# An RNN layer and an LSTM layer in one kernel: a bias load changes its queue, a bias product its place, and the low parts of four weight chunks are made later

## The reference

```python
# layer 0, residual
h = tanh(h @ WhR + (x_t @ WxR + bR));  y_t = x_t + h
# layer 1, residual
a = (y_t @ WxL + bL) + h @ WhL         # 2048 columns: i, f, o, g
c = sigmoid(f) * c + sigmoid(i) * tanh(g)
h = sigmoid(o) * tanh(c);  out_t = y_t + h
```

## Time and profile before

| | us |
|---|---|
| median of 3 runs | 891.57 |
| profiled execution | 892.13 |
| its span | 890.3 |
| TensorE busy | 863.1 (97%) |
| VectorE busy | 746.1 (84%) |
| ScalarE busy | 397.8 (45%) |
| GpSimd busy | 223.4 (25%) |
| granted TensorE clock | 0.997 |

### The profile page before, as it was taken

One profiled execution on the slowest core, in us unless ns is written; L12 is line 12 of the kernel. 1 busy time (PEld: TensorE's weight loads), 2 busy tenths in 40 slices (PEclk: granted clock), 3 DMA queues, 4 the chain that ended last, 5 costly groups with the idle time before them and its releaser, 6 DMA issues.

```text
span 890.3 us, 42241 instructions
## 1 busy us (share of the span) xinstructions
PE 863.1 (97%) x18576; PEld 507.8 (57%) x18576; DVE 746.1 (84%) x1964; ACT 397.8 (45%) x1064; POOL 223.4 (25%) x503
## 2 busy tenths in 40 slices
PE   5999999999999999999999999999999999999996
PEld 4455656555565565555655655555556555565642
DVE  4679888888888888888888888888888888888874
ACT  2746334444444444444444444444444444444431
POOL 1111122222222222222222222222222222222210
PEclk9999999999999999999999999999999999999998
DMA  8901100111100011110011110001111000000000
GB/s 308 264 3 26 27 15 15 26 27 27 27 24 17 16 27 27 27 27 14 15 27 27 27 27 14 22 20 27 27 27 27 15 3 15 15 15 15 15 14 14
DMA packets 38649, 30.06 MB, mean 34 GB/s; under 512 B 4268, under 2 KB 37184, under 8 KB 37184
## 3 DMA queue, kind: packets, MB, share of 16 engines
q1 hardware_dynamic: 38044, 27.16, 10.9%
q10 hardware_dynamic: 420, 0.20, 0.1%
HBM read 18.95 MB, written 8.39 MB: 31 GB/s over the span
## 4 chain that ended last, share of the span: by engine, by line
PE 87%; DVE 6%; DMA 2%; SPq 2%; issue 2%; ACT 1%; POOL 0%; POOLq 0%; DVEq 0%
PE ps_l L783 36%; PE ps_l L809 31%; PE ps_r L848 8%; PE ps_r L865 8%; DMA wxl_raw<-in_L_cond_Wx 2%; PE ps_l L798 2%; SPq L271 1%; DVE pre_l L614 1%; ACT gates L424 1%; DVE h_lo L649 1%; DVE h_hi L636 1%; PE ps_r L823 1%; PE ps_r L833 1%; ACT tanh_c L431 1%; DVE c L625 1%
## 5 line engine op out<-in xcount | busy, mean ns | idle before, releaser
L809 PE MATMUL ps_l<-wxl_hi,whl_raw 128*32 128x512 f16 x3840 | 251.2, 379 | 0.0
L809 PEld LDWEIGHTS ps_l<-wxl_hi,whl_raw 128*32 128x32 f16 x3840 | 104.2, 97 | 103.5 <-issue 4.9
L315 POOL TENSOR_TENSOR xb<-xb,h_l 128x128 f32<-128x128 f32 x128 | 59.2, 462 | 328.4 <-DVE h_l L642 328.4
L783 PE MATMUL ps_l<-whl_hi,hT_hi 128*32 128x512 f16 x2016 | 130.8, 379 | 3.9 <-DVE hT_hi L640 3.1
L338 POOL TENSOR_TENSOR yT<-xT,hT_r 128x128 f32<-128x128 f32 x128 | 58.6, 458 | 295.6 <-DVE hT_r L682 295.6
L783 PE MATMUL ps_l<-whl_hi,hT_lo 128*32 128x512 f16 x2016 | 130.6, 379 | 0.0
L783 PE MATMUL ps_l<-whl_lo,hT_hi 128*32 128x512 f16 x2016 | 130.6, 379 | 0.0
L614 DVE SCALAR_TENSOR_TENSOR pre_l<-ps_l,g_products,bias_l 128x256 f32<-128x256 f32 x240 | 105.1, 479 | 26.1 <-PE ps_l L783 19.5
L809 PE MATMUL ps_l<-wxl_lo,whl_raw 128*32 128x512 f16 x1920 | 125.6, 379 | 0.0
L665 DVE SCALAR_TENSOR_TENSOR pre_r<-ps_r,g_products,xr 64x128 f32<-64x128 f32 x224 | 78.4, 350 | 34.1 <-POOL xr L328 29.1
L436 ACT ACTIVATE h_r<-pre_r 128x128 f32<-128x128 f32 x128 | 39.6, 310 | 134.5 <-DVE pre_r L665 106.6
(11 more groups left out here) (108 smaller groups left out, 1277.4 us busy)
## 6 DMA issues: line engine op xcount, KB each, us to landing
out<-xb SPq DMA_DIRECT2D x128, 64.0 KB, 1.8
xb<-in_x SPq DMA_DIRECT2D x126, 64.0 KB, 2.1
whl_raw<-in_L_cond_Wh SPq DMA_DIRECT2D x4, 1024.0 KB, 14.4
wxl_raw<-in_L_cond_Wx SPq DMA_DIRECT2D x4, 1024.0 KB, 15.9
wxr_raw<-in_L_cond_Wx SPq DMA_DIRECT2D x1, 1024.0 KB, 7.1
whr_raw<-in_L_cond_Wh SPq DMA_DIRECT2D x1, 1024.0 KB, 9.0
xb<-in_x ACTq DMA_DIRECT2D x2, 64.0 KB, 4.8
h0n<-in_cond ACTq DMA_DIRECT2D x1, 64.0 KB
```

The costliest lines, as they stand in the source:

```text
L315: nc.gpsimd.tensor_tensor(xb[g % NX][:, t, :], xb[g % NX][:, t, :], h_l[s % 2][:, :], ALU.add).then_inc(out_done, 1)
L783: last = nc.tensor.matmul(ps_l[s % 2][quarter(j), :], (hT_hi, hT_lo)[h_part][:, k, :], gate_slice(whl[w_part][k], j), start=False, stop=(h ...
L809: last = nc.tensor.matmul(ps_l[s % 2][quarter(j), :], y16[y_part][g % 2][:, k, t * B:(t + 1) * B], gate_slice(wxl[w_part][k], j), start=(y ...
```

## The change

Three edits.

1. The load of the LSTM bias goes from SyncE's queue to ScalarE's, and there the order becomes: two quarters of x, LSTM bias, h0.
2. TensorE does the LSTM bias product right behind the RNN one, ahead of `product_r(0)`; ScalarE waits once, for both, before it copies them.
3. The low parts of the input matrix: chunk 0 in turn 10 instead of 9, chunk 1 in turn 11 instead of 10, chunks 2 and 3 both in turn 12 instead of 11 and 12.

```diff
-        W_LOW_AT = {6: [(OF_H, 1), (OF_H, 2)], 7: [(OF_H, 3)], 9: [(OF_X, 0)], 10: [(OF_X, 1)], 11: [(OF_X, 2)], 12: [(OF_X, 3)]}
+        W_LOW_AT = {6: [(OF_H, 1), (OF_H, 2)], 7: [(OF_H, 3)], 10: [(OF_X, 0)], 11: [(OF_X, 1)], 12: [(OF_X, 2), (OF_X, 3)]}
...
             sp.dma_start(bias_rows_r, bR.rearrange("(j u) -> j u", j=J)).then_inc(s_bias_r, DMA)
-            sp.dma_start(bias_rows_l.rearrange("j (g u) -> j g u", g=G),
-                         bL.rearrange("(g j u) -> j g u", g=G, j=J)).then_inc(s_bias_l, DMA)
             sp.dma_start(wr_raw[OF_X][:, :], WxR.rearrange("(p k) n -> p (k n)", k=J)).then_inc(s_wr[OF_X], DMA)
...
         def _(act):
+            load_x(act, 0, (2, 3))
+            act.dma_start(bias_rows_l.rearrange("j (g u) -> j g u", g=G),
+                          bL.rearrange("(g j u) -> j g u", g=G, j=J)).then_inc(s_bias_l, DMA)
             act.dma_start(h0n[:, :], h0.rearrange("b (j u) -> j b u", j=J)).then_inc(s_h0, DMA)
-            load_x(act, 0, (2, 3))
...
-            act.wait_ge(bias_mm, 1)
+            act.wait_ge(bias_mm, 2)
             nc.scalar.activation(bias_r[:, :], ps_l[0][:, 0:P], ACT.Copy).then_inc(bias_done, 1)
-            act.wait_ge(bias_mm, 2)
             nc.scalar.activation(bias_l[:, :], ps_l[1][:, :], ACT.Copy).then_inc(bias_done, 1)
...
             nc.tensor.matmul(ps_l[0][:, 0:P], spread_j, bias_rows_r, start=True, stop=True).then_inc(bias_mm, 1)
-            product_r(0)
             pe.wait_ge(s_bias_l, DMA)
             nc.tensor.matmul(ps_l[1][:, :], spread_j, bias_rows_l, start=True, stop=True).then_inc(bias_mm, 1)
+            product_r(0)
```

## The result

| | before | after |
|---|---|---|
| median, us | 891.85 (891.12 to 892.18, 4 runs) | 898.58 (897.94 to 898.69, 4 runs) |
| profiled execution, us | 892.13 | 898.72 |
| its span, us | 890.3 | 896.9 |

The ratio is 1.0076, 95% interval 1.0057 to 1.0093: 6.7 us slower, clear of noise, where 1.3 us were forecast, with 894.1 as the upper end of the range.

The account below looks back on a forecast made before the run. The bound was a chain: DMA landing until 38.73 us, TensorE until 97.9, VectorE with ScalarE until 116.5, then TensorE. Terms -0.31 + 0 + 0 + 1.65 = +1.34 us gave a median of 892.9 us, range 891.0 to 894.1.

Parts of the forecast that it names:

- h0's landing: At the front, h0 behind x's quarters and the bias would land at about 9.5 to 10 us, costing nothing.
- the landing at 38.73: At the front, TensorE's `step_0_input` waits until 38.73 us for the last chunk of the LSTM's input matrix.
- Edit 1's gain of 0.31 us: At the front, without the bias load on SyncE's queue the big loads start and land sooner: -0.31 us.
- Edit 2 at 0 us: At the front, the RNN starts about 2 us sooner, but the last input chunk's landing hides it: 0 us.
- turn 9's gain at 0: `cell(4)` could start some 0.3 us sooner, but `cell(5)` cannot, as TensorE's product ends too late: 0 us.
- turn 12's cost of 1.65 us: Two low parts on VectorE delay `y_lo`, TensorE's `product_l(8)` and `cell(7)`: +1.65 us, bounds 0 to 2.27.
- A: Rival, front: the landing isn't set by bytes alone, so 2.07 us more gain comes through; 890.8 us, chance 0.12.
- C: Rival, turn 12: VectorE reaches its two low parts sooner, so their delay vanishes; -0.31 us, 891.3 us, chance 0.08.
- B: Rival, front: the bias load's issue of 0.26 us was hidden, so no gain there; +1.65, 893.2 us, chance 0.14.
- D: Rival, at 97.5 us: TensorE's wait drops its clock to 1.2 GHz, up to 3.6 us more; 896.5, chance 0.04.

Follow-up runs that it names:

- front_only: The changed kernel with the low parts where they were before the change; 896.72 us against 892.06 before.
- h0_on_sync: The changed kernel with low parts as before and h0's load on SyncE's queue ahead of the first 1 MB load; 890.77 us against 891.51 before.
- hold_big: The changed kernel with low parts as before, SyncE waiting for h0 before issuing the first 1 MB load; 892.90 us against 891.51 before.
- order_and_product: The kernel before with x's quarters ahead of h0 on ScalarE's queue and the LSTM bias product ahead of `product_r(0)`; 890.40 us against 891.51.
- order_only: The kernel before with only x's quarters put ahead of h0 on ScalarE's queue; 890.34 us against 892.06 before.
- order_again: The same kernel as order_only, timed again in more rounds; 889.89 us against 891.38 before.
- h0_middle: The changed kernel with low parts as before and ScalarE's queue holding x's quarters, h0, LSTM bias in this order; 893.84 us against 891.38 before.
- low_only: The kernel before with only the low parts moved as in the change; 893.36 us against 892.06 before.
- bias_queue_only: The kernel before with the LSTM bias load moved to ScalarE's queue behind h0 and x's quarters; 891.93 us against 891.38 before.
- low_double_10: The kernel before with low parts 0 and 1 in turn 10, one each in 11 and 12, none in 9; 892.85 us against 891.38 before.
- product_only: The kernel before with only the LSTM bias product put ahead of `product_r(0)`; 892.32 us against 891.51 before.
- h0_first: The changed kernel with h0 issued first on ScalarE's queue, then x's quarters, then the LSTM bias; 894.41 us against 892.06 before.

## Why the prediction was wrong

**The failed step is h0's landing.** I wrote that a quarter of x in that place had landed at 9.41 and "h0 then lands at about 9.5 to 10", and from this that "nothing of this reaches the landing at 38.73". h0 came at 18.35, and a term that the sum held at nothing was +4.99 us at mark 1, +4.66 in front_only's median. Two things were wrong in it. I took over a time of landing from one load to another. What decides it, as far as these runs show, is how much of the queue is still to be fetched when the 1 MB loads begin, and the room that these leave; x's 9.41 was itself such a wait. And I did not see that edit 1 itself moves both ends of the race the wrong way: it puts the bias ahead of h0 (issue at 2.32 us) and starts the first 1 MB load sooner (2.04 instead of 2.45). The runs in one table:

| kernel | h0 issued | first 1 MB load issued | h0 used at |
|---|---|---|---|
| h0_on_sync | 2.03, SyncE | 2.74 | 4.97 |
| hold_big | 2.32 | 5.14 | 5.15 |
| order_and_product | 1.69 | 2.35 | 7.47 |
| order_only | 1.67 | 2.35 | 9.40 |
| order_again | 1.70 | 2.35 | 10.26 |
| h0_middle | 1.68 | 2.02 | 12.98 |
| after | 2.32 | 2.04 | 18.35 |
| front_only | 2.31 | 2.02 | 18.79 |

On ScalarE's queue, issued 0.7 us ahead of the first big load, h0 gets part of its pieces through and comes at 7.5 to 10.3; 0.3 ahead, at 13; behind it, at 18.4 to 18.8. I had cited the Trainium skill, *DMA: Bandwidth & Descriptors*, section "Queues, rings and completion order", which has each DMA engine go round between the queues by packet, and drew from it only that h0 would be late by little. The profile's packets show the size: 26 of q10 against 114 of q1 in 2 us, which isn't one for one.

Only a short stretch of the RNN's delay was free, 1.31 us, and I never asked how much. It would have been the rival to write: RNN steps late by more than the front's cover. I also left out that the peaks of the RNN weights stand behind h0 on VectorE. h0_middle (first recurrent product at 18.09, behind the bias at 14.38) already pays 2.46. Nor was the landing alone the limit of the front before: the chains of low_only, bias_queue_only and low_double_10 begin with x's landing and run through the RNN's steps, not through the last chunk. The two paths were nearly equal there.

**Edit 1's gain of 0.31 us** can't be seen: the first big load was issued 0.41 us sooner, but the stretch behind it was taken over by h0. In bias_queue_only mark 1 came 0.27 sooner and the median 0.55 later; nothing can be told.

**Edit 2 at 0 us** was right: product_only shows no gain, and the product did run in TensorE's idle front (at 4.50). In product_only the first recurrent product came at 12.77, 1.7 us sooner, and TensorE then waited 2.23 us for the last chunk at 39.09.

**Edit 3, turn 9's gain at 0 and turn 12's cost of 1.65 us**, was right. After: +1.60 between the marks; low_only: +1.60 between them and +1.30 in the medians. The wait of the weight loads was 1.79 where 1.63 were forecast, and `y_lo` ended it, as said. Turn 9 went as said too: in low_only `cell(4)` came 19.62 us behind mark 1 instead of 20.01, `cell(5)` 27.40 instead of 27.41.

**The rivals.** A (the RNN's head start comes through) and C (the slip is swallowed) did not happen. B's mechanism was not what cost the front. D fell: behind the wait 16 matmuls took 1.05 us, against 1.04 at 80.70 before. (Its 3.6 us was also a little high: 7.5 us with 1.08 of 1.94 needed loses 3.3.) None of them was the one that came, and the range had no room for it: its upper end was made of the slip alone.

## What to carry to other kernels

A small load on a second queue that the first products need has to be issued well ahead of the big loads of the other queue, or ahead of them in their own queue; otherwise it gets few packets (13 in a microsecond here) and lands several times later than alone (16.0 us against 2.8 here). When loads change places, price each by what will be in flight when it is issued, and count what the edit does to the big loads' start too. A landing that hides a chain covers it only up to a length that has to be read, not assumed.

## What the runs showed of the hardware

- 64 KB in 128 pieces took 2.8 us from issue to use with nothing big in flight, and 16.0 us behind the 1 MB loads of the other queue; 8 KB in 16 pieces took 8.6 us there (h0_first) and 11.5 (h0_middle).
- The first 1 MB load landed 4.9 to 6.5 us behind its issue in the eight kernels with x's quarters first on ScalarE's queue, and 6.4 to 7.7 us behind it in five of the six with h0 first (7.1 before); the sixth, bias_queue_only, has 5.4. By 8 us SyncE's queue had moved 1.42 to 1.55 MB in the four kernels with h0 first and the LSTM bias on SyncE's queue, 1.47 of them before, and 1.65 to 1.94 MB in the others, hold_big aside.
- In order_only the last chunk was in use at 37.30 and in order_again at 36.73 instead of 38.73. The landing alone doesn't make their gain, since in low_double_10, with the loads of before, TensorE had its last wait for a chunk until 37.09. It had reached `step_0_input` at 34.5 to 35.3 us with the front of before (34.87 before, 34.52 in low_double_10, 35.26 in low_only), and reached it at 32.55 in order_only and 32.2 in order_again: the order moves both paths to the front's end.

```profile
16.07 20.62 DMA wxl_raw<-in_L_cond_Wx
36.73 1.06 PE ps_l L761 x8
```

  Why the order of two small loads on one queue moves the start of the stream on the other was not separated: h0's issue took 1.17 us when it came first and x's quarters 0.42 and 0.45, but no run tries one without the other.
- TensorE's granted clock fell to 0.50 (1.2 GHz) for about 3 us in the front of four kernels, front_only from 26 to 29 us and h0_on_sync, hold_big and order_and_product between 27 and 34, with 32 matmuls of 128 columns in 1.94 us instead of 1.08. Before it fell TensorE had been busy for 0.78 us from 22 to 24 (front_only), 0.24 from 24 to 26 (h0_on_sync), 0.65 from 26 to 28 (hold_big) and 0.20 from 24 to 26 (order_and_product). In the last three TensorE still waited 1.4 to 1.5 us for the last chunk, so it did not set the front. In the kernel after the rows give 1.00 throughout, yet 32 matmuls took 1.93 us as late as 24.43; from there to the next `rnn_add` it took 2.00 us against 1.75 before, so slow matmuls are at most a few tenths of the 5 us.
- The same front scatters: h0 in order_only and order_again, the same kernel, came at 9.40 and 10.26.
